# Attention products in runs of two key slots in a fused two-layer kernel

## The reference

```python
h = _layernorm(x, norm_g, norm_b)
Q = h @ wq + bq
K = h @ wk + bk
V = h @ wv + bv
scores = jnp.einsum('bnd,bmd->bnm', Q, K) * scale
attn = jax.nn.relu(scores)                       # no softmax
R = x + jnp.einsum('bnm,bmd->bnd', attn, V)
ffn_out = jax.nn.relu(R @ w1 + b1) @ w2 + b2
return _layernorm(R + ffn_out, fnorm_g, fnorm_b)
```

## Time and profile before

| | us |
|---|---|
| median of 3 runs | 998.52 |
| the runs | 995.6, 998.52, 999.24 |
| span of the profiled execution | 996.3 |
| PE busy / DVE / ACT / POOL | 834.4 / 691.3 / 560.5 / 421.6 |

### The profile page before, as it was taken

One profiled execution on the slowest core, in us unless ns is written; L12 is line 12 of the kernel. 1 busy time (PEld: TensorE's weight loads), 2 busy tenths in 40 slices (PEclk: granted clock), 3 DMA queues, 4 the chain that ended last, 5 costly groups with the idle time before them and its releaser, 6 DMA issues.

```text
span 996.3 us, 17997 instructions
## 1 busy us (share of the span) xinstructions
PE 834.4 (84%) x5574; PEld 594.9 (60%) x5574; DVE 691.3 (69%) x2473; ACT 560.5 (56%) x1259; POOL 421.6 (42%) x441
## 2 busy tenths in 40 slices
PE   5799869999987549934589999999999999999995
PEld 3666646666664436614466676666766667666663
DVE  3758789898866525547767778787777777877542
ACT  1366635555543224412266767777777776777773
POOL 4554477674542620046635553455644453110110
PEclk9599879999986569965579999999999999999998
DMA  9700000000000023310000000000000000000000
GB/s 287 218 12 11 10 14 30 23 24 10 5 4 2 6 89 125 109 40 16 6 2 9 2 7 8 7 8 2 7 9 7 9 2 7 8 7 7 1 12 6
DMA packets 36328, 29.06 MB, mean 29 GB/s; under 512 B 18546, under 2 KB 31770, under 8 KB 35850
## 3 DMA queue, kind: packets, MB, share of 16 engines
q1 hardware_dynamic: 27226, 20.59, 6.8%
q0 software_dynamic: 7200, 5.16, 2.1%
q10 hardware_dynamic: 1808, 2.17, 0.6%
HBM read 16.23 MB, written 15.38 MB: 32 GB/s over the span
## 4 chain that ended last, share of the span: by engine, by line
PE 54%; DVE 8%; ACT 7%; issue 4%; DMA 0%; POOL 0%; ACTq 0%; POOLq 0%; DVEq 0%
PE psum L422 12%; PE psum L862 11%; PE psum L863 7%; PE psum L867 4%; PE psum L868 4%; PE psum L435 3%; PE psum L852 3%; PE psum L1039 2%; ACT L511 2%; ACT L464 1%; ACT scratch L511 1%; PE psum L1021 1%; PE psum L360 1%; DVE stats L1213 1%; PE psum L936 1%
## 5 line engine op out<-in xcount | busy, mean ns | idle before, releaser
L511 ACT ACTIVATE scratch<-psum,fb 128x292 f32<-128x292 f32 (+1 forms) x512 | 227.2, 490 | 51.3 <-PE psum L863 50.1
L862 PE MATMUL psum<-xs,fw_hi 128*128 128x292 f32 (+1 forms) x512 | 180.4, 362 | 27.7 <-ACT scratch L511 27.7
L862 PEld LDWEIGHTS psum<-xs,fw_hi 128*128 128x128 f32 x512 | 98.3, 192 | 88.2 <-ACT scratch L511 56.0
L422 PE MATMUL psum<-scratch,w_fw 128*64 128x292 f32 (+1 forms) x1024 | 148.6, 412 | 0.0
L863 PE MATMUL psum<-xs,fw_lo 128*128 128x292 f32 (+1 forms) x512 | 144.9, 293 | 0.0
L302 POOL DMA_INDIRECT uu<-expert_out,slot_i x80 | 84.1, 1051 | 68.7 <-DVE stats L1213 42.5
L852 PE MATMUL psum<-w_ident,hl 128*128 128x128 f32 (+1 forms) x400 | 72.9, 300 | 36.6 <-DVE hl L1222 26.3
L863 PEld LDWEIGHTS psum<-xs,fw_lo 128*128 128x128 f32 x512 | 99.6, 194 | 0.0
L815 POOL DMA_INDIRECT slots_buf<-hl,slot_i x80 | 79.7, 997 | 43.5 <-issue 26.3
L519 ACT ACTIVATE yt<-psum,w_fb 128x256 f32<-128x256 f32 (+1 forms) x128 | 62.6, 489 | 61.8 <-PE psum L422 61.8
L422 PEld LDWEIGHTS psum<-scratch,w_fw 128*64 128x64 f32 x1024 | 62.9, 138 | 42.6 <-issue 12.8
(11 more groups left out here) (289 smaller groups left out, 1996.6 us busy)
## 6 DMA issues: line engine op xcount, KB each, us to landing
slots_buf<-zeros SPq DMA_DIRECT2D x8, 704.0 KB, 8.0
scratch<-slots_buf SPq DMA_DIRECT2D x8, 704.0 KB, 4.4
expert_out<-scratch SPq DMA_DIRECT2D x8, 352.0 KB, 2.5
out<-H SPq DMA_DIRECT2D x16, 128.0 KB
X<-in_patches ACTq DMA_DIRECT2D x1, 1728.0 KB, 7.8
slots_buf<-hl,slot_i POOLq DMA_INDIRECT x80
uu<-expert_out,slot_i POOLq DMA_INDIRECT x80, 2.3
scratch<-in_fw SPq DMA_DIRECT2D x1, 1024.0 KB
```

Source lines behind the costliest of these rows:

```text
L422: last = pe.matmul(bank(6)[h * D:(h + 1) * D, 0:z - a], w["fw2"][:, (2 * p + h) * J + j, :], hid[(4 * n + 2 * j + h) % 8][:, 0:z - a], sta ...
L511: act.activation(hid[m % 8][:, 0:z - a], bank(up_bank(m))[:, 0:z - a], ACT.Gelu, bias=fb1[:, e * J + j:e * J + j + 1]).then_inc(sem("gelu" ...
L862: pe.matmul(dst, parts[0][:, cols], rhs, start=True, stop=False)
```

## The change

The place of `attend` in the loop over s is taken from a table. Slots 0 and 1 are issued at s = 2, slots 2 and 3 at s = 4, slot 4 at s = 5, each after the other work of that s. Scores, relu and all other engines' programs stay as they are, and so does the order in which the slots are added up.

```diff
         STEPS = NB + LAG["scatter"]
         WEIGHTS_STEP = 9
+        RUNS = {2: (0, 1), 4: (2, 3), 5: (4,)}
...
-                    if A is not None and s >= 1:
-                        attend(A, s - 1)
+                    if A is not None:
+                        for t in RUNS.get(s, ()):
+                            attend(A, t)
```

## The result

The change made the kernel slower. In one comparison on one chip the median went from 998.88 to 1011.83 us, a ratio of 1.0145 with a 95% interval of 1.0121 to 1.0169. The forecast was 995.1 with a range up to 999.5: it was wrong in sign and left the time outside. Two of the signs that the prediction had named for its being wrong appeared: L1336 (L1338 in the changed kernel) waits for ACT, and TensorE runs at 1.2 GHz between 150 and 250 us.

A forecast was written before the change was run, and what follows sets the result against it. DVE was taken as the full engine in the middle steps, PE's chain in the last. Stage terms 0 - 0.3 + 0 - 0.8 - 1.1 = -2.2, clock -1.2: 998.5 - 3.4 = 995.1 us, range 991.0 to 999.5.

The forecast's parts named there:

- signs that the prediction had named for its being wrong: Steps 6 to 12 shorter, L1336 waiting for L1115 there, or TensorE at 1.2 GHz between 150 and 250 us.
- What a run costs: One slot's products alone cost PE 0.86 us, a second in the same run 0.49; each removed run saves 0.37.
- `y_turn`: From sequence 4 on, PE reaches it about 0.7 us early, stands waiting for ACT's `t3` copy, and starts it as before.
- Covers of sequences 6 to 12: DVE-bound steps: delays stay within DVE's slack and PE's wait before L960, so 0 us (range -0.5 to +0.7).
- Sequences 0 to 3: PE-bound steps: at most +0.1 us each, a vanishing `t2` wait offsets; together 0 (range -0.4 to +0.7).
- Sequences 4 and 5: `ffn1`'s delay lets relu and POOL's subtractions start earlier in step 5, ending it 0.2 to 0.3 us early (0 to -0.7).
- Sequences 13 to 15: Steps on PE's chain of waits: -0.8 us for 13 and 14 together, -1.1 for 15.
- rival 3: No gain: POOL's subtraction catches DVE's next instruction instead, and sequence 15 is carried by POOL; 998.3 us, 11%.
- The clock: The 10.2 us stretch at 1.2 GHz from 293.1 us may be spared: 3.7 us more, valued at a third, -1.2.
- rival 4: Slower: new stand before `y_turn` lets the clock fall in full-clock steps, 4.1 us per stretch; 1004.5 us from two, 7%.
- ends of the range: Below, lower ends with the clock dip spared whole, -7.5 (991.0 us); above, all upper ends, +1.0 (999.5).

The follow-up runs named there:

- e3: The changed kernel with slot 0's products also computed one extra time in their old place (after `t3`), result overwritten; 999.34 us, ratio 1.0022.
- e4: The changed kernel with six extra full-height 8-column matmuls in slot 0's old place, result overwritten; 1008.58 us, ratio 1.0123.
- e12: Against the kernel before, only slots 2 and 3 joined, the other slots in their old places; repeated on another chip; 1000.47 us, ratio 1.0032.
- e1: Against the kernel before, only slots 2 and 3 joined; slots 0, 1 and 4 in their old places; 1000.7 us, ratio 1.003.
- e2: Against the kernel before, only slot 0 moved, into a run with slot 1; 1021.27 us, ratio 1.0227.
- e8: Against the kernel before, slots 0 to 3 each one place later, slots 3 and 4 in one run; 1032.22 us, ratio 1.0240.
- e10: The changed kernel itself, run again on another chip; 1012.64 us, ratio 1.0163 to the kernel before.
- v1: Against the kernel before, only slots 3 and 4 joined, after `ffn1`; slots 0, 1 and 2 in their old places; 993.71 us, ratio 0.9988.
- v2: Against the kernel before, slots 1 and 2 joined after `v`, slots 3 and 4 after `ffn1`, slot 0 alone in its old place; 994.55 us, ratio 0.9980.
- e11: The changed kernel with slot 0's products also computed once in their old place, repeated on another chip; 1001.32 us, ratio 1.0065.
- v3: Slots 1 and 2 joined, 3 and 4 joined, slot 0 in its old place, against the kernel before; repeated on another chip; 1015.74 us, ratio 1.0012.
- e6: The changed kernel with four extra full-height 292-column matmuls in slot 0's old place, result overwritten; median 1006.03 us, ratio 1.0085.
- e7: The changed kernel with only the left 256 columns of slot 0's products computed an extra time in the old place; 1029.89 us, ratio 1.0169.
- e5: The changed kernel with slot 0's products computed one extra time after `k`, directly ahead of the pair of slots 0 and 1; 1008.48 us, ratio 1.0086.
- e9: The changed kernel with slot 0's products computed one extra time after `k`, repeated on another chip; 1032.51 us, ratio 1.0232.

## Why the prediction was wrong

**What a run costs: right.** L937 stands in 47 runs. The pair in e3 takes 187.58 - 186.44 = 1.14 to the next start, that is 0.64 + 0.50 against the forecast 0.49. So the work was saved as said.

**`y_turn`: right.** In the changed kernel it waits for ACT's L1166 and starts 2.08 us after `t3` (204.76 - 202.68), as before: 196.36 - 194.29 = 2.07 in the trace of before. The stand is 0.34, not 0.7: the scores ahead of it start 0.90 behind `t3` instead of 1.41, so 0.5 earlier, and last a little longer.

**Covers of sequences 6 to 12: right, where the clock stays up.** The fall-free step in e4, ACT and then DVE:

```profile
209.18 0.72 ACT L1125 ACTIVATE kh<-psum,bk 128x548 fp32r<-128x548 f32 x1
```
```profile
210.26 0.79 DVE L1346 SCALAR_TENSOR_TENSOR kl<-psum,bk,kh 128x548 fp32r<-128x548 f32 x1
```

The slack of `k_high` is 210.26 - 209.18 - 0.72 = 0.36; the forecast was 0.86 - 0.49 = 0.37. PE's wait for `place` shrinks to 0.55, forecast "about 0.5":

```profile
199.81 0.71 PE L967 MATMUL psum<-ff,w_w 128*64 128x256 f32 x4 [0.55 <-DVE carry L1442]
```

**Sequences 0 to 3: right but for 0.** 1 to 3 sum to +0.1 (+0.21, -0.08, -0.07). Sequence 0 grew by 1.32; the clock came up at 49.9 us there instead of 47.3.

**Sequences 4 and 5: open.** The forecast was 0.2 to 0.3 less for both together. The changed kernel has falls in both. In e12 the step of sequence 4 has none and took 16.05 us against 15.56 before, 0.49 more. Whether sequence 5 gives that back is not shown, since every trace has a fall in it.

**Sequences 13 to 15: 14 covered over, 15 right in kind.** The undisturbed sizes are in e1: -0.6 in 13 and in 14, where the same removed run was forecast to bring -0.4 each. The changed kernel itself has -0.11 in 13 and a fall in 14. From sequence 15 on the 6.1 us that come back stand against a forecast of 1.1, or 4.8 with the fall of the earlier trace rows spared (1.1 + 3.7). The long DVE instruction beside POOL (L1379 in the earlier trace rows) moved on to the next line there, as rival 3 described. In the chain of the changed kernel:

```profile
285.91 0.51 DVE zt L1379
286.44 2.44 DVE zt L1381
```

**The clock: the step that failed.** The term that failed is rival 4, new falls in steps that ran at 2.4 GHz, which the forecast counted as nothing. The prediction gave this part one dip to spare (-1.2) and weighed its opposite, rival 4, at 7% with the sentence that "PE's idle sits in two smaller places instead of one, and its longest shrinks". Both are true in the trace and neither decided. In the 3.4 us ahead of the fall at 206.9, PE was busy 3.01 of 3.41; ahead of the fall of the earlier trace rows it had been busy 1.91 of 3.40, and I took the idle for the cause. I never asked what PE was busy with, and whether the change took the heaviest piece out of the lightest stretch. From `q` to the end of `k` the two kernels differ by one thing, slot 0's products. PE is busy 5.22 of 5.41 us before and 4.82 of 5.41 after; 0.34 of the 0.40 missing is the stand before `y_turn`. The rows are of before and then of after:

```profile
193.30:198.71 5.41, 5.22 (x36) 3.81 (x35) 4.45 (x25) 3.83 (x11) 2.44 (x4) 1.00 0.05 12
```
```profile
201.70:207.11 5.41, 4.82 (x31) 3.68 (x30) 4.44 (x25) 3.79 (x11) 2.33 (x3) 0.98 0.08 15
```

The Trainium skill, "TensorE: Matmul & The Clock Gate", section "HAM oscillation", explains a return of the lower clock by waits that leave the engine idle. e4 speaks against reading only that from it here: with this stand filled, falls still came (0.93 of the clock, ratio 1.0123).

Rival 4's price was right, its count was not. It had 4.1 us per 10.2 us at the lower level, 0.40 per us. In sequences 0 to 14 the time at the lower level grew from 27 to 74 us and the steps by 18.6 us: 18.6 / 47 = 0.40 per us. Up to the last `place`, with the fall of sequence 15 gone, it grew from 77 to 110 us for 12.3 us lost, 0.37 per us. With the right amount, 33 x 0.40 - 2.2 = +11.0, the forecast would have been 1009.5. Its range was given as if the clock could do harm in no more than 7 of 100 cases. The ends of the range are added up slightly wrong as well: the terms give -8.3 and +1.1 where the text has -7.5 and +1.0. Nothing hangs on that.

**Shown, and open.** Shown: the loss goes with the granted clock; it appears when slot 0's products leave their place (e2, e8, e10), stays at least in part with light work there (e4), and goes largely when they are put back, truly (e1, e12, v1, v2) or as waste (e3, e11). It is neither the delay of slot 3's scores (e3) nor the number of runs (v2, v3). Open: which property of the stretch the chip answers to (e6 is undecided, e7 has no partner on its chip, e5 kept its clock without slot 0 there), what share the new stand before `y_turn` has, and what differs between chips and executions.

## What to carry to other kernels

Before moving a heavy piece of TensorE's work, look at what stays behind: a stretch of transposes and narrow matmuls may have kept its clock by that one piece, though PE looks busy with or without it. Here the profile of before had three falls between 50 and 305 us, and a reordering made them eleven. Where a profile shows even a few, the schedule may be near such an edge: price 10 us more at the lower clock (4 us here) as a case with a real chance, and compare it to the gain. Work that fills another engine's waiting time may be doing a second service.

## What was not expected of the hardware

A kernel with more work was faster: 1001.32 us with 16 extra runs of 0.86 us, 1012.64 without. One program (e5, e9) lay at 1000 to 1011 us in four of its six executions on one chip and at 1029 to 1038 on another, with mean clocks of 0.894 to 0.902 and 0.876 to 0.880, while the kernel before went from 997.0 to 1012.25. On that second chip steps without a fall were longer too, 17.35 and 17.55 us against 16.64 in one and the same kernel (v3, v2), which the TensorE clock does not explain. In those two steps of v3, DVE stood 1.2 us each before L1376 (a reciprocal that follows ACT's root) with nothing to wait for that the profile shows; in the two of v2 it did not.
